# The second normalisation of a gated cross-attention and expert kernel by ScalarE, router logits in column groups, and five changes of order around them

## The chip, the cores and the metric

One core of a Trainium2 chip runs the kernel as one program. Its engines are TensorE (PE, matmuls and transposes; PEld is its weight load), VectorE (DVE), ScalarE (ACT), GpSimd (POOL) and SyncE (SP), which here only issues DMAs. Each runs its own list of instructions in order and waits on semaphores for the others. The metric is the time of the whole program on the device in microseconds.

## What is computed

For 16 sequences of 256 tokens of width 256, `x` is first changed by gated cross-attention to a context, and then by a gated layer of experts. From the reference, with the settings of the parts left out:

```python
x = x + tanh(g_xattn) * attention(layernorm(x), ctx, ctx, Wq, bq, Wk, bk, Wv, bv, Wo, bo)   # 16 heads of 16
x = x + tanh(g_ffn) * experts(layernorm(x), ...)

logits = xf @ w_router                                   # 8 experts
scores = softmax(logits); weights, indices = top_k(scores, 2)
y = (silu(xf @ w1[e]) * (xf @ w3[e])) @ w2[e]            # hidden width 512
moe_out = sum over the two experts of weight * y
shared = (silu(xf @ ws1) * (xf @ ws3)) @ ws2
out = shared / 3 + moe_out * 2 / 3
```

## The kernel before

Every large product is made of three matmuls on a high and a low part of its operands (`high*high`, `low*high`, `high*low`), so each tensor that goes into a matmul is first split: ScalarE copies the high part, VectorE or GpSimd subtracts and leaves the low part.

**Attention** is software-pipelined over the sequences, called batches here: b0 to b15. In iteration i (from -4 to 15) batch i+4 (`Eb`) is read and its first normalisation is begun, i+3 (`A`) is projected to k, q and v, i+2 (`F`) goes through DRAM and comes back as rows of `q4` and `k4`, for i+1 (`B`) the row maxima of the scores are found, i (`C`) has its scores again and their exponentials, i-1 (`S`) is divided and turned, i-2 (`S2`) is projected out, added to `x` and normalised a second time, i-3 (`S3`) is routed, and i-4 (`S4`) gets its places in the lists of the experts. An iteration has eight slots p = 0 to 7, each for one pair of heads: on TensorE four matmuls of scores for the exponential (`scores_to_exp`), four for the maximum (`scores_to_max`), and then that slot's share of the other stages. VectorE takes one `row_max` of 128 by 1024 in each slot, with `before(p)` ahead of it and `behind(p)` after it; ScalarE takes one exponential of 128 by 1024 (L953) in each slot, with a `before` and a `behind` too. The order in each slot is written out by hand, and nothing reorders it.

What the change touches in an iteration:
- `logits` (L705, slot 1): eight matmuls of 128 rows by 8 columns of output into bank `T1`. On VectorE `best_two` in slot 2 finds the two best experts, and `masks` (L1265 to L1269) behind that slot's `row_max`. `rank` (L715, L716, slot 3) counts into `T2`, and `positions` (L1273) reads the counts behind slot 4.
- `residual` (L1299), `residual_stats` (L1231) and `residual_variance` (L1237, L1242) of `S2` in slots 4 and 5 on VectorE; the root of the variance (L1653) on GpSimd; `norm` (L1314, two `tensor_scalar` of 128 by 256) on VectorE in slot 7; `turn_norm` (L650) on TensorE at the end of slot 7.
- `turn_max` (L681) turns the 16 maxima per token in slot 0, ScalarE negates them into `mT` (L1008), and SyncE writes them as the 64th row of each half of `q4`.
- GpSimd subtracts the mean of `Eb` (L1707), multiplies by the root (L1710), then takes the root of `S2` and leaves the low part of q (`leave_low`, L1685).

**The ramp** (i < 0) has no work of later stages; there TensorE also runs `keep_warm`, matmuls whose output nobody reads (L604). SyncE's list (`half_out` stores q or k of a batch to DRAM, `terms_in` reads them back) is written out for the first three batches.

**Behind the iterations** stands a tail for b14 and b15, woven into tiles 0 to 5 of the shared expert. Then tiles 6 and up: at most 48 routed tiles (it depends on the routing) of 256 tokens, in loops, and the rest of the shared tiles, mixed into the output. `scatter` writes each token's normalised row to the lists of its two experts in DRAM (`xs_d`), and `clear_behind` (L341) writes 512 rows of zeros behind each list's end, 514 KB for each of eight lists. SyncE clears list 0, reads the first routed tile, clears 2, 4 and 6, and reads the second tile; GpSimd clears 1, 3, 5 and 7 (counted on `z_pool`). SyncE reads a tile with four DMAs (`load_tile`, L442); `turn_rows` (L1422) on VectorE turns it, and `xg_h` and `xg_l` are its two parts. Only the first four routed tiles are read before all of the clears are known to be done.

## Time and profile of the kernel before

| | |
|---|---|
| median of three runs | 816.92 us (815.06 to 818.07) |
| the profiled execution's own time | 814.12 us |
| its span, granted clock of TensorE | 812.4 us, 0.992 of full speed |
| busy: TensorE, weight load | 769.9 us (95%), 686.5 us (85%) |
| busy: VectorE, ScalarE, GpSimd | 538.8 us (66%), 413.4 us (51%), 430.7 us (53%) |
| chain that ended last | PE 61%, POOL 10%, DMA 9%, issue 7%, DVE 7%, ACT 4% |

The busy share is an average over stages that differ. In the trace the first exponential scores of batch i mark iteration i: the ramp takes about 60 us, the iterations in the middle some 20 to 21 us each up to about 355 us, the tail and the first shared tiles last to about 425 us, the routed tiles to about 700 us, and the remaining tiles to the end. The time of a part is read as the distance between the same instruction in two iterations, and a loss as the idle time that stands in brackets at the instruction that waited.

### The profile page before, as it was taken

The page shows a single profiled execution, that of the slowest core. Times are in us where ns is not written, and L with a number is a line of the kernel's source. Part 1 is how long each engine was busy: PE and PEld are TensorE (multiplying, and loading weights), DVE is VectorE, ACT ScalarE, POOL GpSimd, SP SyncE. Part 2 cuts the span into 40 slices and gives each one's busy share as a digit, 9 for nine tenths or more (in the row PEclk, how much of TensorE's full clock was granted, in tenths as well). Part 3 has the DMA queues.
Part 4 walks back from the last instruction along what each step waited for, and adds up shares of the span by engine and source line. Part 5 has one row for each costly group of instructions (what it writes and reads, how often), then busy time and mean ns, then how long its engine had stood idle before and what let it go on. Part 6 is the DMA issues. An engine that isn't in the chain of part 4 may idle for free.

```text
span 812.4 us, 19406 instructions
## 1 busy us (share of the span) xinstructions
PE 769.9 (95%) x6955; PEld 686.5 (85%) x6956; DVE 538.8 (66%) x1118; ACT 413.4 (51%) x690; POOL 430.7 (53%) x489
## 2 busy tenths in 40 slices
PE   4888999999999998898997999999999999999998
PEld 3756777777777776578997999999999999999998
DVE  5677889998888888857644444444444444446897
ACT  5667777777777767653324333333334334333332
POOL 5633446666666654457772476656756675236000
PEclk9999999999999999999998999999999999999999
DMA  6854557776666654244394354444543422317622
GB/s 213 272 179 158 173 185 231 234 235 209 210 209 209 198 182 145 93 170 138 110 248 113 96 155 130 117 114 131 142 116 78 111 70 58 72 53 306 233 93 79
DMA packets 129150, 127.34 MB, mean 157 GB/s; under 512 B 55232, under 2 KB 111040, under 8 KB 129088
## 3 DMA queue, kind: packets, MB, share of 16 engines
q1 hardware_dynamic: 114896, 80.34, 33.4%
q0 software_dynamic: 14192, 46.19, 16.9%
q8 instruction: 37, 0.61, 0.3%
q14 instruction: 25, 0.20, 0.1%
HBM read 75.32 MB, written 50.91 MB: 155 GB/s over the span
## 4 chain that ended last, share of the span: by engine, by line
PE 61%; POOL 10%; DMA 9%; issue 7%; DVE 7%; ACT 4%; SPq 2%; POOLq 1%; ACTq 0%; DVEq 0%
PE bank L562 7%; PE bank L563 6%; PE bank L564 6%; PE bank L643 6%; PE bank_ss L614 6%; PE bank_sm L627 4%; POOL w_l L1635 4%; DMA y_d<-y_s,y_rows 3%; PE bank_sm L562 3%; PE bank_ss L562 3%; PE bank_sm L563 3%; PE bank_sm L564 3%; PE bank_ss L564 3%; PE bank_ss L563 3%; PE bank L650 3%
## 5 line engine op out<-in xcount | busy, mean ns | idle before, releaser
L1248 DVE TENSOR_REDUCE row_max<-bank_sm 128x4 f32<-128x1024 f32 x124 | 151.5, 1222 | 37.8 <-PE bank_sm L627 36.2
L953 ACT ACTIVATE probs_T<-bank_ss 128x1024 f32<-128x1024 f32 x123 | 126.5, 1028 | 18.9 <-PE bank_ss L614 17.9
L1227 DVE TENSOR_TENSOR gT_l<-gg,gT_h 128x1024 fp32r<-128x1024 f32 x49 | 66.8, 1363 | 102.0 <-ACT gT_h L1084 100.1
L562 PE MATMUL bank_sm<-xg_h,w_h 128*128 128x256 f32 x400 | 114.3, 286 | 7.1 <-DVE xg_l L1227 7.1
L562 PE MATMUL bank_ss<-xg_h,w_h 128*128 128x256 f32 x400 | 113.2, 283 | 0.5 <-DVE gg L1434 0.5
L563 PE MATMUL bank_sm<-xg_h,w_l 128*128 128x256 f32 x400 | 113.6, 284 | 0.0
L564 PE MATMUL bank_sm<-xg_l,w_h 128*128 128x256 f32 x400 | 113.5, 284 | 0.0
L564 PE MATMUL bank_ss<-xg_l,w_h 128*128 128x256 f32 x400 | 112.9, 282 | 0.0
L563 PE MATMUL bank_ss<-xg_h,w_l 128*128 128x256 f32 x400 | 112.9, 282 | 0.0
L562 PE MATMUL bank<-w_h,gT_h 128*128 128x256 f32 x392 | 111.1, 284 | 1.5 <-DVE gT_l L1227 1.5
L563 PE MATMUL bank<-w_h,gT_l 128*128 128x256 f32 x392 | 110.9, 283 | 0.0
L564 PE MATMUL bank<-w_l,gT_h 128*128 128x256 f32 x392 | 110.7, 282 | 0.0
L1685 POOL TENSOR_TENSOR qk_s<-qk_s 128x512 fp32r<-128x512 f32 x32 | 41.8, 1307 | 108.9 <-ACT qk_s L994 108.9
L562 PEld LDWEIGHTS bank_sm<-xg_h,w_h 128*128 128x128 f32 x400 | 77.2, 193 | 8.1 <-DVE xg_l L1227 7.6
L1761 POOL DMA_INDIRECT y_d<-y_s,y_rows x68 | 73.5, 1081 | 17.1 <-issue 16.5
L563 PEld LDWEIGHTS bank_sm<-xg_h,w_l 128*128 128x128 f32 x400 | 77.2, 193 | 0.0
L564 PEld LDWEIGHTS bank_sm<-xg_l,w_h 128*128 128x128 f32 x400 | 77.1, 193 | 0.0
L562 PEld LDWEIGHTS bank_ss<-xg_h,w_h 128*128 128x128 f32 x400 | 76.3, 191 | 0.8 <-DVE gg L1434 0.8
L1078 ACT ACTIVATE sg<-bank_sm 128x512 f32<-128x512 f32 x98 | 53.2, 595 | 46.6 <-PE bank_sm L564 46.6
L994 ACT ACTIVATE qk_s<-bank,bqk_s 128x256 f32<-128x256 f32 (+1 forms) x128 | 53.5, 481 | 45.8 <-PE bank L564 45.8
L562 PEld LDWEIGHTS bank<-w_h,gT_h 128*128 128x128 f32 x392 | 74.8, 191 | 2.1 <-DVE gT_l L1227 2.1
L563 PEld LDWEIGHTS bank_ss<-xg_h,w_l 128*128 128x128 f32 x400 | 76.4, 191 | 0.0
(204 smaller groups left out, 1945.6 us busy)
## 6 DMA issues: line engine op xcount, KB each, us to landing
qk_d<-qk_s SPq DMA_DIRECT2D x64, 256.0 KB, 2.8
w_raw<-wall POOLq DMA_DIRECT2D x27, 512.0 KB
k<-qk_d SPq DMA_DIRECT2D x48, 256.0 KB
q<-qk_d SPq DMA_DIRECT2D x48, 256.0 KB
xq<-xs_d SPq DMA_DIRECT2D x140, 64.0 KB
y_pairs<-y_d POOLq DMA_DIRECT2D x16, 512.0 KB, 9.7
x<-x SPq DMA_DIRECT2D x16, 256.0 KB, 4.7
c_s<-ctxT SPq DMA_DIRECT2D x16, 256.0 KB, 3.1
```

The source lines that it names most:

```text
L562: pe.matmul(out, ah, bh, start=first and k == 0, stop=False)
L563: pe.matmul(out, al, bh, start=False, stop=False)
L564: r = pe.matmul(out, ah, bl, start=False, stop=last and k == n - 1)
L614: r = pe.matmul(exp_bank(V.b, pv)[:, par * 512 + half * L:par * 512 + (half + 1) * L], k4[V.slot][own, pv, half * P:(half + 1) * P], q4[V. ...
L643: r = pe.matmul(OT[g % 2][PVW * i:PVW * (i + 1), :], v_s[V.v_slot][:, kc, h, :], pT[:, h % 8, kc * L:(kc + 1) * L], start=kc == 0, stop=kc ...
L953: act.activation(pT[:, 2 * (pv % 4):2 * (pv % 4) + 2, :].rearrange("p h t -> p (h t)"), exp_bank(V.b, pv)[:, :], ACT.Exp, scale=D ** -0.5) ...
L994: r = act.activation(dst.bitcast(F32) if half else dst, bnk[:, oc * L:(oc + 1) * L], ACT.Identity, bias=bqk_s[:, 2 * side + oc:2 * side + ...
L1078: r = act.activation(sg[:, 2 * n:2 * n + 2, :].rearrange("p f t -> p (f t)"), psH1[n][:, :], ACT.Silu)
L1227: return v.tensor_tensor(dst, ps, high.bitcast(F32), ALU.subtract)
L1248: v.tensor_reduce(mx[B.slot][:, :, :].rearrange("p t (r q) -> p r t q", r=2)[:, :, :, p], max_bank(B.b, p)[:, :].rearrange("p (r t k) -> p ...
L1685: po.tensor_tensor(rest, rest.bitcast(F32), high.bitcast(F32), ALU.subtract).then_inc(done, 1)
L1761: po.indirect_dma_start(out=yd, out_offset=bass.IndirectOffsetOnAxis(ap=to[:, t:t + 1].bitcast(U32), axis=0), in_=y_s[:, t, :], in_offset= ...
```

## The change

- **The second normalisation** of batches 0 to 12 goes from VectorE to ScalarE: `x * rstd + shift`, an `Identity` with a pointer for scale and one for bias, behind slot 7. VectorE makes `-mean` (128 by 2) with the variance, GpSimd multiplies it by the root (`norm_terms`), and both of GpSimd's steps now stand between its subtraction and its multiplication for `Eb`. `turn_norm` goes to slot 0 of the next iteration.
- **The logits of batches 0 to 9** (iterations 3 to 12): the router's weights are padded to 32 columns and become the stationary side; four matmuls of 128 columns, one for each pair of chunk and token half, write four column groups of `T1`. ScalarE copies the bank (128 by 128), and one matmul by a matrix of zeros and ones (`C_SEL`) in slot 2 adds the halves and turns them back. `best_two`, `masks` and `rank` of these batches come a slot later, `rank` into `T0`; `attention_rows` in slot 5 then waits for `pos_ok`, which for all batches stood ahead of q's projection before.
- **The ramp**: of b0, GpSimd leaves the low part of q ahead of its multiplication, and SyncE reads q back ahead of b1's stores of k. The maxima of b0 are turned and written in two halves (`turn_first`, `first_max`, `first_rows`), and 14 + 4 + 4 matmuls of `keep_warm` become 4. The bias of the projection out is made an iteration earlier, a clear of `v` an iteration later.
- **The tail**: on VectorE the variance and `norm` of b14 stand ahead of b13's `positions`; GpSimd's order scatter, root, cut becomes cut, root, scatter (`cut` splits a part of the next expert weights).
- **The clears**: SyncE does all. Lists 1 and 2 are cleared where 2, 4 and 6 were, lists 3 to 7 one by one after every other routed tile in an unrolled part of its loop. GpSimd's clears go.

```diff
-CW = C_T3 + NST
+C_SEL = C_T3 + NST
+CW = C_SEL + TC * NX
+LW = P // (TC * EC)
+THIN = NB - AHEAD - 2
...
+            def first_rows(half):
+                sp.wait_ge(mT_ok, half + 1)
+                for par in range(2):
+                    row = ROWS * par + MROW
+                    sp.dma_start(q4[0][row:row + 1, HALF * half:HALF * half + HALF, :].bitcast(F32),
+                                 first_mT[half][par:2 * HALF:2, :].bitcast(F32)).then_inc((first_mrow, mrow)[half], 16)
...
             load_x(Batch(3))
+            terms_in(b0, 0)
             half_out(b1, 1)
-            terms_in(b0, 0)
             load_c(Batch(3))
+            terms_in(b1, 1)
             half_out(b1, 0)
-            terms_in(b1, 1)
             load_x(Batch(4))
             terms_in(b1, 0)
+            first_rows(0)
             half_out(b2, 1)
+            half_out(b2, 0)
+            first_rows(1)
             terms_in(b2, 1)
-            half_out(b2, 0)
-            max_rows(b0)
             terms_in(b2, 0)
...
-            clear_behind(sp, (2, 4, 6), z_done)
+            clear_behind(sp, (1, 2), z_done)
...
-            with sp.Fori(1, last3) as u:
+            for u in range(1, 2 * NX - 5):
+                if u % 2 and u > 1:
+                    sp.wait_ge(z_done, 16 * ((u + 3) // 2))
+                load_routed(u + 3)
+                load_rows(u)
+                if u % 2 and (u + 5) // 2 < NX:
+                    clear_behind(sp, ((u + 5) // 2,), z_done)
+            sp.wait_ge(z_done, 16 * (NX - 1))
...
+            def logits_apart(S3):
+                if among_first(S3, 1):
+                    pe.wait_ge(few_in, 64)
+                pe.wait_ge(xn2T_ok, S3.n(1, 1))
+                for j in range(TC * EC):
+                    t, k = j // EC, j % EC
+                    r = pe.matmul(lgT_p[LW * j:LW * (j + 1), :], wr_s[:, k, :], xn2T[:, k, t * P:(t + 1) * P], start=True, stop=True)
+                r.then_inc(lgT_ps, 1)
+
+            def logits_joined(S3):
+                pe.wait_ge(lgT_ok, S3.n(1, 1))
+                pe.matmul(lg_thin, lgT_s[:, :], K[:, C_SEL:C_SEL + TC * NX], start=True, stop=True).then_inc(lg_ps, 1)
...
-                        keep_warm(SS[:, 0:512], 14)
-                    if B and B.b == 1 and p == 1:
                         keep_warm(SS[:, 0:512], 4)
+                    if B and among_first(B, 1) and p == HALF + 1:
+                        pe.wait_ge(xnTl_ok, A.n(1, 1))
+                        turn_first(0)
                     if B:
                         scores_to_max(B, p)
+                    if p == 0 and C and among_first(C, 1):
+                        turn_first(1)
                     if p == 0 and C and not among_first(C, 1):
                         turn_max(C, S2)
+                    if p == 0 and S3 and by_scalar(S3):
+                        turn_norm(S3)
                     if p == 0 and S:
                         values(S, 2)
                     if p == 1 and S3:
-                        logits(S3, lg_p)
+                        (logits_apart if thin(S3) else logits_whole)(S3)
...
                         values(S, 3)
+                    if p == 2 and S3 and thin(S3):
+                        logits_joined(S3)
...
-                    if p == 3 and S3:
+                    if p == 3 and S3 and not thin(S3):
...
+                    if p == 4 and S3 and thin(S3):
+                        pe.wait_ge(xnTl_ok, A.n(1, 1))
+                        rank(S3, rk_thin)
                     if p == 4 and C:
...
+                        if S3:
+                            pe.wait_ge(pos_ok, S3.n(1, 1))
                         if C:
-                            pe.wait_ge(mT_ok, C.n(1, 1))
+                            pe.wait_ge(mT_ok, C.n(1, 2))
                         attention_rows(S)
                     if p == 5 and A:
...
-                        turn_norm(S2)
-                if B and among_first(B, 1):
-                    pe.wait_ge(mx_ok, PAIRS - 1)
-                    keep_warm(SM[:, 0:512], 4)
-                    turn_max(B, None)
...
+            def norm(S2):
+                act.wait_ge(shift2_ok, S2.n(1, 1))
+                moved(act, sc_done[1], S2.n(32, 32 - R * 32))
+                for t in range(TC):
+                    r = act.activation(xn2_s[S2.slot][:, t, 0:E], x2_s[:, t, :], ACT.Identity, bias=shift2[:, t:t + 1], scale=rstd2[:, t:t + 1])
+                r.then_inc(xn2_ok, 1)
...
+            def logits_turned(S3):
+                act.wait_ge(lgT_ps, S3.n(1, 1))
+                moved(act, lg_ps, S3.n())
+                act.activation(lgT_s[:, :], lgT_p, ACT.Copy).then_inc(lgT_ok, 1)
...
-                    if p == 0 and C:
-                        act.wait_ge(mT_ps, C.n(1, 1))
+                    if p == 0 and C and among_first(C, 1):
+                        first_max(1)
+                    if p == 0 and C and not among_first(C, 1):
+                        act.wait_ge(mT_ps, C.n(1, 2))
+                        act.wait_ge(first_mrow, 32)
                         moved(act, mrow, C.n(32))
                         act.activation(mT[:, :], mT_p, ACT.Copy, scale=-1.0).then_inc(mT_ok, 1)
+                    if p == HALF + 1 and i == -1:
+                        first_max(0)
...
+                    if p == 7 and S2 and by_scalar(S2):
+                        norm(S2)
...
+                if mv is bmv2:
+                    v.tensor_scalar(mean2[:, :], mv[:, :, 0], -1.0, None, ALU.mult)
                 v.tensor_scalar(mv[:, :, 1], mv[:, :, 1], 1e-5, None, ALU.add).then_inc(done, 1)
...
-                    if p == 2 and S3:
+                    if p == 2 and S3 and not thin(S3):
                         best_two(S3, lg_p)
+                    if p == 3 and S3 and thin(S3):
+                        best_two(S3, lg_thin)
...
-                    if p == 2 and S3:
+                    if p == 2 and S3 and not thin(S3):
                         masks(S3)
                     if p == 3 and A:
                         v.wait_ge(xnTh_ok, A.n(1, 1))
                         low(xnT_l[:, :, :], bank_chunks(T0), xnT_h[:, :, :]).then_inc(xnTl_ok, 1)
+                    if p == 3 and S3 and thin(S3):
+                        masks(S3)
...
             residual_stats(x14)
+            residual_variance(x14)
+            norm(x14)
             positions(x13, rk_tail)
-            residual_variance(x14)
             list_slots(x13)
             divide(x15)
-            norm(x14)
...
+                def norm_terms():
+                    root(bmv2, rstd2, var2_ok, S2, rstd2_ok)
+                    if by_scalar(S2):
+                        po.wait_ge(rstd2_ok, S2.n(1, 1))
+                        po.tensor_tensor(shift2[:, :], mean2[:, :], rstd2[:, :], ALU.mult).then_inc(shift2_ok, 1)
...
+                    if A and among_first(A, 1):
+                        leave_low(0, qh_ok, ql_ok)
+                    if S2:
+                        norm_terms()
                     po.wait_ge(rstd1_ok, Eb.n(1, 1))
                     po.wait_ge(xc_ok, Eb.n(1, 1))
                     po.tensor_tensor(xn_s[:, :, :], xn_s[:, :, :], rstd[:, :].unsqueeze(2).to_broadcast([P, TC, E]), ALU.mult).then_inc(xn_ok, 1)
...
-                    root(bmv2, rstd2, var2_ok, S2, rstd2_ok)
-                if A:
+                if S2 and not Eb:
+                    norm_terms()
+                if A and not among_first(A, 1):
                     leave_low(0, qh_ok, ql_ok)
                 if i == NB - 1:
...
-            scatter(Batch(NB - 4), 1)
             po.wait_ge(oh_ok, x13.n(1, 1))
             po.wait_ge(exp_ok, NB * PAIRS)
             po.wait_ge(mx_ok, NB * PAIRS)
+            cut(1, 0, which=(0,))
             root(bmv2, rstd2, var2_ok, x14, rstd2_ok)
-            cut(1, 0, which=(0,))
+            scatter(Batch(NB - 4), 1)
             scatter(x13, 0)
             scatter(x13, 1)
```

What this does to the lists of instructions, at three places. **VectorE, slots 2 to 5 of iteration 3** (S3 is b0; `row_max_1` are the maxima, `xnT_l` a low part for q, `one_hot` to `mask_total` the masks, `x2_s` the residual, `list_pos` the positions). Before:

```order
L1248 TENSOR_REDUCE row_max_1<-bank_sm 128x2x2 [waits sm_ps]
L1265 TENSOR_TENSOR one_hot<-consts,logits_order 128x32 [waits lgc_ok]
L1268 TENSOR_TENSOR mask<-one_hot 128x16 [waits chain]
L1269 TENSOR_TENSOR mask_total<-mask_total,mask 128x8 [waits chain]
L1248 TENSOR_REDUCE row_max_1<-bank_sm 128x2x2 [waits sm_ps]
L1227 TENSOR_TENSOR xnT_l<-bank6,xnT_h 128x512 [waits xnTh_ok]
L1299 SCALAR_TENSOR_TENSOR x2_s<-bank7,gate_tanh,x_0 128x512 [waits x2_st,xb_ok,op_ps]
L1248 TENSOR_REDUCE row_max_1<-bank_sm 128x2x2 [waits sm_ps]
L1231 BN_STATS bn_st2<-x2_s 128x6 [waits x2_ok]
L1231 BN_STATS bn_st2<-x2_s 128x6
L1273 TENSOR_TENSOR list_pos<-bank5,consts 128x16 [waits rk_ps]
```

After, from slot 3 on:

```order
L1344 TENSOR_REDUCE row_max_1<-bank_sm 128x2x2 [waits sm_ps]
L1321 TENSOR_TENSOR xnT_l<-bank6,xnT_h 128x512 [waits xnTh_ok]
L1361 TENSOR_TENSOR one_hot<-consts,logits_order 128x32 [waits lgc_ok]
L1364 TENSOR_TENSOR mask<-one_hot 128x16 [waits chain]
L1365 TENSOR_TENSOR mask_total<-mask_total,mask 128x8 [waits chain]
L1395 SCALAR_TENSOR_TENSOR x2_s<-bank7,gate_tanh,x_0 128x512 [waits x2_st,xb_ok,op_ps]
L1344 TENSOR_REDUCE row_max_1<-bank_sm 128x2x2 [waits sm_ps]
L1325 BN_STATS bn_st2<-x2_s 128x6 [waits x2_ok]
L1325 BN_STATS bn_st2<-x2_s 128x6
L1369 TENSOR_TENSOR list_pos<-bank6,consts 128x16 [waits rk_ps]
```

The masks moved from behind slot 2's maximum to behind slot 3's and the low part, right ahead of the residual.

**TensorE, slots 4 and 5 of the same iteration** (`bank_ss` and `bank_sm` are the scores, L643 / L682 the values, L659 / L698 `attention_rows`). Before, from the end of `rank`, which stands ahead of slot 4's scores:

```order
L716 MATMUL bank5<-mask,counters 128x16
L614 MATMUL bank_ss<-q4_1,k4_1 128x256 [waits exp_ok]
L614 MATMUL bank_ss<-q4_1,k4_1 128x256 x3
L627 MATMUL bank_sm<-k4_2,q4_2 128x256 [waits mx_ok]
L627 MATMUL bank_sm<-k4_2,q4_2 128x256 x3
L643 MATMUL bank4<-probs_T,v_0 32x256 [waits ot_ok,exp_ok,vr_ok]
L643 MATMUL bank4<-probs_T,v_0 32x256 x7
L614 MATMUL bank_ss<-q4_1,k4_1 128x256 [waits exp_ok]
L614 MATMUL bank_ss<-q4_1,k4_1 128x256 x3
L627 MATMUL bank_sm<-k4_2,q4_2 128x256 [waits mx_ok]
L627 MATMUL bank_sm<-k4_2,q4_2 128x256 x3
L659 MATMUL bank6<-consts,oT_1 128x128 [waits mT_ok,ot_ok,x2_ok,xnTl_ok]
```

After:

```order
L666 MATMUL bank_sm<-k4_2,q4_2 128x256 [waits mx_ok]
L666 MATMUL bank_sm<-k4_2,q4_2 128x256 x3
L777 MATMUL bank6<-mask_total,counters 128x16 [waits acc_ok,oh_ok,xnTl_ok]
L778 MATMUL bank6<-mask,counters 128x16
L682 MATMUL bank4<-probs_T,v_0 32x256 [waits ot_ok,exp_ok,vr_ok]
L682 MATMUL bank4<-probs_T,v_0 32x256 x7
L651 MATMUL bank_ss<-q4_1,k4_1 128x256 [waits exp_ok]
L651 MATMUL bank_ss<-q4_1,k4_1 128x256 x3
L666 MATMUL bank_sm<-k4_2,q4_2 128x256 [waits mx_ok]
L666 MATMUL bank_sm<-k4_2,q4_2 128x256 x3
L698 MATMUL bank6<-consts,oT_1 128x128 [waits mT_ok,pos_ok,ot_ok,x2_ok,xnTl_ok]
```

`rank` moved behind both groups of scores of slot 4 and ahead of the values, and `attention_rows` waits for `pos_ok` as well.

**SyncE, in the ramp**, from the stores of b0's q on (`q4_0` are b0's rows of q; the two stores with `k_high_ok` and `kl_ok` are those of b1's k). Before:

```order
L396 DMA qk_d<-qk_s 128x2x256 [waits q_high_ok]
L396 DMA qk_d<-qk_s 128x2x256 [waits ql_ok]
L363 DMA x_3<-x 128x2x256 [waits var1_ok]
L396 DMA qk_d<-qk_s 128x2x256 [waits k_high_ok,k_high_st]
L396 DMA qk_d<-qk_s 128x2x256 [waits kl_ok,k_low_st]
L407 DMA q4_0<-qk_d 32x8x256 [waits q_high_st,q_zero0]
L407 DMA q4_0<-qk_d 32x8x256
L407 DMA q4_0<-qk_d 32x8x256 [waits q_low_st]
```

After:

```order
L416 DMA qk_d<-qk_s 128x2x256 [waits q_high_ok]
L416 DMA qk_d<-qk_s 128x2x256 [waits ql_ok]
L383 DMA x_3<-x 128x2x256 [waits var1_ok]
L427 DMA q4_0<-qk_d 32x8x256 [waits q_high_st,q_zero0]
L427 DMA q4_0<-qk_d 32x8x256
L427 DMA q4_0<-qk_d 32x8x256 [waits q_low_st]
L416 DMA qk_d<-qk_s 128x2x256 [waits k_high_ok,k_high_st]
L416 DMA qk_d<-qk_s 128x2x256 [waits kl_ok,k_low_st]
```

The three reads of b0's q moved ahead of the two stores of b1's k.

## Rows read from the trace of the kernel before

**Rows 1.** Timeline (start, length, instruction, idle before, releaser): VectorE and TensorE at tile 7.
```profile
429.05 0.73 DVE L1422 STREAM_TRANSPOSE bank<-xq 128x512 f32<-128x512 f32 x1 [10.19 <-DMA xq<-xs_d]
...
431.19 0.58 PE L562 MATMUL bank_sm<-xg_h,w_h 128*128 128x256 f32 x1 [6.10 <-DVE xg_l L1227]
```

**Rows 2.** Windows: length; busy PE, PEld, DVE, ACT, POOL (count); clock, DMA share, GB/s.
```profile
412.00:416.00 4.00, 4.00 (x36) 4.00 (x35) 2.70 (x5) 0.60 (x1) 2.89 (x3) 1.00 1.09 289
432.00:436.00 4.00, 4.00 (x24) 4.00 (x24) 2.43 (x8) 3.59 (x6) 0.00 (x0) 0.64 0.53 165
436.00:440.00 4.00, 4.00 (x36) 4.00 (x35) 1.79 (x6) 2.15 (x4) 0.00 (x0) 1.00 0.18 35
```

**Rows 3.** DMA issues with KB each and median us to landing: the clears.
```profile
xs_d<-zero_rows SPq DMA_DIRECT2D x4, 514.0 KB, 7.2
xs_d<-zero_rows POOLq DMA_DIRECT2D x4, 514.0 KB, 13.1
```

**Rows 4.** Waits between 431 and 700 us: total, times, longest.
```profile
ACT y_s L1094 <- DMA y_d<-y_s,y_rows: 59.7, 16, 5.2
```

**Rows 5.** Chain of waits, 20 to 32 us: start, length, what.
```profile
25.04 5.33 DMA q<-qk_d
```

**Rows 6.** Timeline of the ramp: GpSimd, then TensorE.
```profile
19.47 1.28 POOL L1685 TENSOR_TENSOR qk_s<-qk_s 128x512 fp32r<-128x512 f32 x1
...
30.42 0.51 PE L627 MATMUL bank_sm<-k,q 63*128 63x256 f32 x4 [1.56 <-DMA q<-qk_d]
...
41.33 1.19 PE L604 MATMUL bank_sm<-wt_h 128*128 128x512 f32 x4 [0.64 <-DVE row_max L1248]
```

**Rows 7.** Windows, columns as in rows 2: iterations 4, 8 and 12.
```profile
120.12:141.28 21.16, 20.56 (x210) 15.40 (x208) 19.40 (x48) 14.79 (x29) 14.21 (x17) 1.00 0.71 226
203.18:223.32 20.14, 19.77 (x210) 15.20 (x208) 17.98 (x48) 14.80 (x29) 13.29 (x17) 1.00 0.63 211
283.82:304.75 20.93, 20.12 (x210) 15.30 (x209) 18.51 (x42) 14.45 (x28) 10.78 (x14) 1.00 0.52 177
```

**Rows 8.** Timeline of TensorE, iteration 9, slots 1 and 5.
```profile
222.65 0.51 PE L614 MATMUL bank_ss<-q,k 64*128 64x256 f32 x4 [0.37 <-issue]
...
223.32 1.06 PE L705 MATMUL bank<-wr_s,xn2T 128*128 128x8 f32 x8
...
232.98 1.09 PE L659 MATMUL bank<-consts,oT 128*128 128x128 f32 x8
```

**Rows 9.** Timeline of VectorE, iteration 9, slots 2 to 5.
```profile
227.76 0.18 DVE L1265 TENSOR_TENSOR one_hot<-consts,logits_order 128x32 f32<-128x32 f32 x1
...
228.87 1.23 DVE L1248 TENSOR_REDUCE row_max<-bank_sm 128x4 f32<-128x1024 f32 x1 [0.52 <-PE bank_sm L627]
...
231.27 1.22 DVE L1248 TENSOR_REDUCE row_max<-bank_sm 128x4 f32<-128x1024 f32 x1
...
233.06 0.16 DVE L1273 TENSOR_TENSOR list_pos<-bank,consts 128x16 f32<-128x16 f32 x1
```

**Rows 10.** Timeline: VectorE beside GpSimd's work, and without (237.64).
```profile
135.29 1.70 DVE L1314 TENSOR_SCALAR xn<-x_s,bn_mv,rstd 128x256 f32<-128x256 f32 x2 [0.45 <-POOL rstd L1653]
...
237.64 0.73 DVE L1314 TENSOR_SCALAR xn<-x_s,bn_mv,rstd 128x256 f32<-128x256 f32 x2
...
293.98 1.72 DVE L1242 TENSOR_SCALAR bn_mv<-bn_mv 128x2 f32<-128x2 f32 x1
```

**Rows 11.** Timeline of ScalarE: two halves with one pointer; the maxima's copy.
```profile
205.78 0.84 ACT L994 ACTIVATE qk_s<-bank,bqk_s 128x256 fp32r<-128x256 f32 x2 [1.67 <-PE bank L564]
...
221.32 0.37 ACT L1008 ACTIVATE minus_max_T<-bank 16x256 fp32r<-16x256 f32 x1 [0.83 <-PE bank L681]
```

**Rows 12.** Timeline of the tail: VectorE, then TensorE.
```profile
364.08 2.45 DVE L1314 TENSOR_SCALAR xn<-x_s,bn_mv,rstd 128x256 f32<-128x256 f32 x2 [0.50 <-POOL rstd L1653]
...
366.58 0.66 PE L650 MATMUL bank<-consts,xn 128*128 128x128 f32 x4 [1.09 <-DVE xn L1314]
368.25 0.39 PE L562 MATMUL bank_sm<-xg_h,w_h 128*128 128x256 f32 x1 [1.01 <-DVE xg_l L1227]
```

85 lines of the change are left out of this document (55 added, 30 removed).

## The prediction

> **What bounds the kernel now.** I read the busy shares first: TensorE is busy 95% of the span and no other engine is over 66%. So time can come only from TensorE's idle stretches, its slow clock, and its own work. I then went through TensorE's timeline by stage. The largest idle stretch of the program is 6.10 us, ahead of the first matmul of the second routed tile [rows 1]. The ramp has a wait of 1.56 us at its first scores and shorter ones later [rows 6]. The tail has two of about 1 us [rows 12]. In the iterations TensorE is busy 19.77 us of 20.14 in iteration 8; iterations 4 and 12 take 21.16 and 20.93 [rows 7]. VectorE is busy 17.98 us of the same 20.14, most of it in row maxima that feed the next scores, so small delays there reach TensorE.
>
> All sums are made against the profiled execution's own 814.12 us, which is 2.80 under the median of 816.92. I add that back at the end.
>
> **The clears: -7.1.** VectorE turned the second routed tile 10.19 us late, because the tile's read had not landed; TensorE stood still until 431.19 [rows 1]. All eight clears were in the queues by then, eight times 514 KB, with a median landing of 7.2 and 13.1 us [rows 3]. The read was issued at about 413 behind them. After the change only three clears come ahead of it (lists 0, 1 and 2), all issued some 5 us or more before it. I expect the read to land at 417 to 420, against about 423 from which it would be in time, so the whole 6.10 goes. The clock also fell in the pause: in the four microseconds after, TensorE began 24 matmuls, and 36 in the four after those [rows 2]. That is 4 x 12/36 = 1.3 us lost, and about 0.4 more ahead of that window: 1.7. Together -7.8; with the landing late by a little, -6.
>
> The other five clears now go one by one between the reads of routed tiles. A clear keeps the DMA engines busy for about 1.8 us by the 289 GB/s that stand at 412 to 416, where the clears ran [rows 2] (an estimate: 514 KB over that rate), once in two tiles of 8.6 us. ScalarE there already waits for the results' writes, 59.7 us in 16 waits [rows 4], and this was no cost to TensorE, whose longest pause in that stage was 0.6 us; but the cushion is not shown to be large. I take +0.7 for the five, between 0 and +3.
>
> **The ramp: -3.9.** TensorE's first scores of b0 waited 1.56 us at 30.42 for the last read of q, which landed 5.33 us after its issue at 25.04 [rows 5, 6]. Ahead of it stood 14 `keep_warm`, which were over by then. The low part of q is left by GpSimd; the first half's subtraction at 19.47 took 1.28 [rows 6] and stood behind a multiplication, which the change puts after it. The reads also no longer queue behind two stores of b1's k, of 256 KB each. I estimate the last landing at 27.5: -2.9. At the end of b0's maxima TensorE ran four more `keep_warm` after an idle 0.64 [rows 6] and then turned the maxima; VectorE idled 0.4 us in the meantime. Both groups of matmuls go, and VectorE passes from b0's last maximum straight to b1's first: -1.0. What comes late next is the k of b3: ScalarE's copy overwrites what the store of b2's k reads, and that store now stands behind `first_rows(0)`. By the times of this trace it lands at 41.3 to 42, needed by 42.9, so it is just hidden. Bounds: -1.1 (only the GpSimd part) to -5.5 (with the clock, which fell for 3.6 us here, kept up).
>
> **Iterations 3 to 12: -2.8.** I walked iteration 9. On TensorE: `logits` took 1.06 us for eight matmuls [rows 8]. The four column groups have no row of their own. The nearest is four matmuls of 256 columns in two row groups, 0.51 [rows 6]; half the columns gives 0.25. I take 0.28, from 0.25 to 0.5. The joining matmul is one of eight such, a quarter of 1.06 at most: +0.25. So k's projection starts 0.64 earlier, and slot 3's scores 0.39 earlier.
>
> On VectorE the third maximum starts at 228.48 and not at 228.87, where it had idled 0.52 [rows 9]. The masks, 0.60 in all from 227.76 on [rows 9], move behind that maximum and the low part. They end at 230.82, the residual at 231.39, and the fourth maximum starts there and not at 231.27 [rows 9]. `rank` must wait for the masks: TensorE is ready for it at 230.55 and gets them at 230.85. Its lead falls from 0.60 to 0.06. Then `positions` ends at about 233.34, `attention_rows` waits for it until 233.40 and not 232.98 [rows 8]: +0.42. The idle 0.37 ahead of slot 1's scores [rows 8] takes most of that up. The period stays 20.2, and TensorE's saving is not cashed. In the six iterations like iteration 8 I take +0.2 in sum.
>
> Where the change pays is in iterations that VectorE disturbs. The 128 by 256 pair of `norm` takes 0.73 alone, but 1.70 beside a GpSimd subtraction at 135.29, after an idle 0.45 on the root [rows 10]. Iterations 4 to 6, in which GpSimd takes its longest operations, lasted 62.87 together (the first of them 21.16 [rows 7]); with the pair and its wait gone from VectorE I put them at 60.6, -2.3. In iteration 12 the small addition at 293.98 took 1.72 beside a GpSimd addition of 128 by 512 [rows 10]. GpSimd's own work in that stretch moves: 20.93 [rows 7] to 20.2, -0.7.
>
> ScalarE takes the norm. The nearest row is a pair of 128 by 256 with one pointer, 0.84 [rows 11]; I take 0.95. It stands behind slot 7, ahead of the copy of the maxima, which had idled 0.83 before it [rows 11], so it fits almost exactly. If it does not, slot 0's exponential comes later by what is over, 0.1 to 0.4 each. VectorE's new 128 by 2 operation costs 0.17 in slot 5; GpSimd's extra one lies where it idles. `turn_norm` only moves from slot 7 to slot 0. Sum: 0.2 - 2.3 - 0.7 = -2.8, from -7.8 to +1.
>
> The Trainium skill, in "Advanced Engine Details and Errata", section "Mode Summary", states that VectorE's faster modes and GpSimd hold a shared port against each other. The trace agrees with it: 0.73 alone and 1.70 beside GpSimd. By that rule the excess leaves with the norm, but the new small operation may pay it in its place, and iteration 12 would keep its 1.5.
>
> The same notes, "ScalarE: Activation LUTs", section "What ACT_TABLE_LOAD costs", give a price for an activation and for each pointer. By it the pair would take an estimated 1.08 us; the sum would be higher by at most 0.5.
>
> **Iterations 13 to 15: +0.4,** for `turn_norm` in slot 0 of the first of them and for the wait on `pos_ok`.
>
> **The tail: -1.6.** VectorE's norm of b14 took 2.45 us at 364.08 beside `cut`; TensorE waited 1.09 for it and 1.01 for the tile behind it [rows 12]. With the variance and the norm first, and `cut` done before, the norm ends by about 362.5, and both waits shrink to about 0.5 in all. Bounds -0.5 to -2.2.
>
> **Sum.** -7.8 + 0.7 - 3.9 - 2.8 + 0.4 - 1.6 = -15.0. 814.1 - 15.0 = 799.1, and with the 2.8 back **802**.
>
> **The rivals.**
> - *TensorE sets the pace of the iterations* (0.15). The saving of 0.5 us in ten iterations is cashed. For it speaks that TensorE is busy 98% of iteration 8; against it the walk above, where `rank` and `attention_rows` wait for VectorE. 802 - 5 = 797.
> - *The ramp gives nothing* (0.15). Without `keep_warm` the clock falls at b0's scores, or the read of q is slow from the traffic beside it, as its 5.33 us suggest. 802 + 3.9 = 806.
> - *The pause at the clears returns elsewhere* (0.10). The read of a routed tile, or the results' writes, queue behind a clear in the loop, and five tiles lose 1 to 1.5 us each; ScalarE's waits for those writes speak for it. 802 + 7 = 809.
> - *No gain that can be told* (0.06). Ramp and clears both fail: 802 + 3.9 + 7.8 = 814.
> - *Slower* (0.04). The chain masks, residual, fourth maximum, fifth maximum on VectorE becomes the bound, because `best_two` now needs a gap ahead of slot 3's maximum. VectorE has 2.2 us of idle time in iteration 8. If `best_two` misses its gap, the output projection waits too (it needs `lgc_ok`), and a full slot of about 2.5 us is lost. It decides from 1.5 us in each of ten iterations; at 2.5 it gives 802 + 2.8 + 25 = 830. Against it: the logits come half a microsecond earlier, and a whole slot lies between.
> - That the change does not do what it says can hold for the norm: if ScalarE is late for the maxima, the row-maximum chain starts late. It is priced above at 0.1 to 0.4 an iteration, +1 to +5, within the range.
>
> **How the numbers follow.** My forecast has 0.50. The range of 796 to 810 covers it with its own bounds (-6 to -7.8, 0 to +3, -1.1 to -5.5, -7.8 to +1) and the first three rivals, less their edges. A measurement of this kernel can tell about 0.5%, 4 us. Faster by more than that, under 812.8: 0.90; within: 0.06; slower: 0.04.
>
> **What would show it.** Right: no idle stretch ahead of the second routed tile and full clock behind it; b0's first scores at about 27.5; the same matmul 20.2 us apart in all of iterations 4 to 12, with waits of TensorE for `one_hot`/masks at `rank` and for `list_pos` at `attention_rows`; ScalarE's norm pair at 0.95; the tail's two waits under 0.6 together. Wrong: periods of 19.7 or less (then TensorE set the pace), periods over 20.5 (then VectorE's or ScalarE's chain did), a low clock between 25 and 40 us, or waits for reads in the first ten routed tiles.

## The result, and the profile after

The changed kernel takes 809.78 us (median of 7 runs, 807.48 to 813.55) against 816.99 us (7 runs, 815.06 to 819.48). The ratio is 0.9914, with a 95% interval of 0.9887 to 0.9941: 0.9% faster, where 1.8% was forecast. The profiled execution took 807.48 us (span 805.6) against 814.12 (span 812.4).

The gain is split by matmuls that stand in both programs. "Batch i" is the second group of scores for the exponential of batch i, in slot 3 of iteration i (batch 1's is what the expectations below call slot 1 of iteration 1); "tile" is the first matmul of that tile. A period is the distance between two such marks.

| stretch | before | after | change | forecast |
|---|---|---|---|---|
| start to batch 1 (ramp) | 66.03 | 66.55 | +0.5 | -3.9 |
| batch 1 to 2 | 18.49 | 18.53 | 0.0 | |
| batch 2 to 12 (iterations 3 to 12, nearly) | 204.07 | 204.37 | +0.3 | -2.8 |
| batch 12 to tile 0 | 69.47 | 69.87 | +0.4 | +0.4 |
| tile 0 to 4 (tail) | 41.08 | 40.39 | -0.7 | -1.6 |
| tile 4 to 8 (clears) | 42.40 | 34.42 | -8.0 | -7.8 |
| tile 8 to the last matmul | 367.84 | 368.50 | +0.7 | +0.7 |

The row behind batch 12 holds the rest of iteration 12. Measured from its slot 1 to the next one, that iteration went from 20.9 to 20.4 us: -0.5, where the forecast of -2.8 counted on -0.7.

The clears gave what was forecast, and the other parts together nothing. Here is the stretch of the changed kernel in which TensorE had stood still and run slowly [rows 1, 2]; the columns are length, busy PE, PEld, DVE, ACT and POOL, granted clock, DMA share and GB/s:

```profile
424.00:428.00 4.00, 4.00 (x35) 4.00 (x35) 2.12 (x4) 2.29 (x3) 2.81 (x4) 1.00 0.99 281
428.00:432.00 4.00, 4.00 (x36) 4.00 (x35) 2.72 (x11) 3.83 (x8) 0.00 (x0) 1.00 0.32 118
```

TensorE begins 35 and 36 matmuls in 4 us, at full clock. In the routed tiles ScalarE's waits for the results' writes grew from 59.7 us in 16 [rows 4] to 63.0 in 17, with no new pause of TensorE to be seen (0.47 us was its longest behind tile 8, 0.57 before):

```profile
ACT y_s L1188 <- DMA y_d<-y_s,y_rows: 63.0, 17, 5.1
```

**The ramp** after (timelines give start, length, instruction, and in brackets the idle time before it and its releaser):

```profile
28.52 0.51 PE L666 MATMUL bank_sm<-k,q 63*128 63x256 f32 x4 [2.95 <-DMA q<-qk_d]
...
40.67 0.50 PE L666 MATMUL bank_sm<-k,q 63*128 63x256 f32 x4 [1.76 <-DMA q<-qk_d]
...
42.50 0.51 PE L666 MATMUL bank_sm<-k,q 63*128 63x256 f32 x4 [0.98 <-DVE row_max L1344]
...
42.00:47.00 5.00, 4.50 (x26) 4.00 (x27) 2.77 (x9) 1.09 (x3) 0.00 (x0) 0.66 0.66 206
```

The last read of b0's q lands 1.9 us earlier than in [rows 5, 6], not 2.9. But TensorE then pauses again, ahead of b1's scores (40.67) for b1's q, and at 42.50 for VectorE, and 26 matmuls behind these pauses run at a mean clock of 0.66. In the kernel before this stretch had 33 matmuls and full clock:

```profile
42.00:47.00 5.00, 4.78 (x33) 3.20 (x33) 4.32 (x11) 0.61 (x2) 0.53 (x1) 1.00 0.60 187
```

The wait for b1's q comes from the new order of SyncE's list. The store of b1's q stands behind the read of b1's k now, where it stood ahead of it, and so the three reads of b1's q are issued 3.9 us later. Before, and after:

```profile
31.84 1.90 SPq L407 DMA_DIRECT2D q<-qk_d  x3
```
```profile
35.70 1.90 SPq L427 DMA_DIRECT2D q<-qk_d  x3
```

**Iteration 8 to 9** after, TensorE:

```profile
203.49 0.42 PE L764 MATMUL bank<-xn2T,wr_s 128*32 128x128 f32 x8
...
207.11 0.40 PE L769 MATMUL bank<-consts,logits_T 128*128 128x16 f32 x2
...
210.50 0.41 PE L666 MATMUL bank_sm<-k,q 63*128 63x256 f32 x4
211.15 0.25 PE L777 MATMUL bank<-mask_total,counters 128*128 128x16 f32 x1 [0.24 <-issue]
...
213.82 0.95 PE L698 MATMUL bank<-consts,oT 128*128 128x128 f32 x7 [0.38 <-issue]
```

(The program has four matmuls of logits in either kernel. With fp32 operands each stands as two in the trace, which is why the rows count eight, here and in [rows 8], and two for the joining one.)

VectorE at the same place, and ScalarE's norm:

```profile
210.45 0.18 DVE L1361 TENSOR_TENSOR one_hot<-consts,logits_order 128x32 f32<-128x32 f32 x1
...
210.88 0.17 DVE L1365 TENSOR_TENSOR mask_total<-mask_total,mask 128x8 fp32r<-128x8 f32 x1
...
213.45 0.16 DVE L1369 TENSOR_TENSOR list_pos<-bank,consts 128x16 f32<-128x16 f32 x1
...
220.32 1.15 ACT L1048 ACTIVATE xn<-x_s,shift,rstd 128x256 f32<-128x256 f32 x2
```

As forecast, the counts (L777) wait for the masks (`mask_total` at 210.88) and `attention_rows` (L698) for the positions (213.45 + 0.16). The first wait is 0.24, the second 0.38 (0.42 was forecast), and the idle 0.37 of [rows 8] is gone. But the period is 20.38, not 20.2, in each of the six between batches 6 and 12, where it was 20.17 before in all but the first. The windows of one period, before and after:

```profile
207.93:228.09 20.16, 19.79 (x210) 15.21 (x209) 18.03 (x48) 14.80 (x28) 13.34 (x16) 1.00 0.63 209
```
```profile
207.92:228.31 20.39, 19.77 (x212) 14.83 (x211) 17.21 (x47) 15.87 (x32) 13.39 (x17) 1.00 0.62 201
```

VectorE is busy 0.8 us less and ScalarE 1.1 more, and TensorE loses 0.2.

In iterations 4 to 6 the gain is 0.7 in all (62.14 against 62.88 from batch 4 to 7) and not 2.3, the period before them is 0.7 longer (20.91 against 20.19), and the one before that 0.8 shorter (19.41 against 20.17). VectorE no longer has a norm that GpSimd could hold up, but in iterations 3 and 5 a small operation now meets GpSimd's work, and the masks come late for the counts, which waited 0.76 us in iteration 3:

```profile
106.64 1.04 POOL L1813 TENSOR_TENSOR xn_s<-x,bn_mv 128x512 f32<-128x512 f32 x1
107.02 0.70 DVE L1361 TENSOR_TENSOR one_hot<-consts,logits_order 128x32 f32<-128x32 f32 x1
...
143.95 0.51 PE L651 MATMUL bank_ss<-q,k 64*128 64x256 f32 x4 [0.59 <-DMA q<-minus_max_T]
...
146.64 1.00 DVE L1357 TENSOR_TENSOR logits_less_max<-logits_sorted 128x16 f32<-128x16 f32 x1
147.57 1.21 DVE L1344 TENSOR_REDUCE row_max<-bank_sm 128x4 f32<-128x1024 f32 x1
...
146.33 1.28 POOL L1785 TENSOR_TENSOR qk_s<-qk_s 128x512 fp32r<-128x512 f32 x1 [4.49 <-ACT qk_s L1079]
...
149.99 0.25 PE L777 MATMUL bank<-mask_total,counters 128*128 128x16 f32 x1 [0.56 <-issue]
```

The 128 by 16 subtraction took 1.00 us in place of 0.15 (at 208.13, without GpSimd beside it), and the counts waited 0.56 in place of 0.24. In iteration 5 of this profile TensorE also waited 0.59 us for the row of the maxima to land (143.95). The run with the filled ramp, whose iterations have the same code, had the first of these waits (0.64) and not the second.

The Trainium skill ("Advanced Engine Details and Errata", section "Mode Summary") states that GpSimd and VectorE's two-port instructions block each other; of a `tensor_tensor` such as this one that section says nothing. The runs here show that the excess came and went with the overlap, and not whether a port is the reason.

### The profile page after: what moved, and what is told of

Read it like the earlier page. It is cut to its first block, busy times and chain, and to the rows that moved or that the text cites. A ratio compares the mean times of both kernels' runs of the same rounds, so it can differ in the third digit from the quotient of the medians.

```text
span 805.6 us, 19417 instructions
## 1 busy us (share of the span) xinstructions
PE 764.6 (95%) x6959; PEld 679.4 (84%) x6960; DVE 523.9 (65%) x1108; ACT 427.8 (53%) x727; POOL 428.3 (53%) x498
## 4 chain that ended last, share of the span: by engine, by line
PE 64%; DMA 10%; POOL 9%; issue 7%; DVE 6%; ACT 2%; SPq 1%; POOLq 1%; ACTq 0%; DVEq 0%
PE bank L597 7%; PE bank L682 7%; PE bank L598 6%; PE bank L599 6%; PE bank_ss L651 6%; PE bank_sm L666 4%; DMA y_d<-y_s,y_rows 4%; PE bank_sm L597 4%; PE bank_ss L597 3%; PE bank_sm L598 3%; PE bank_sm L599 3%; PE bank_ss L599 3%; PE bank_ss L598 3%; POOL w_l L1735 3%; PE bank L689 2%
## 5 line engine op out<-in xcount | busy, mean ns | idle before, releaser
L1867 POOL DMA_INDIRECT y_d<-y_s,y_rows x68 | 70.2, 1032 | 16.4 <-issue 15.9
L599 PEld LDWEIGHTS bank_ss<-xg_l,w_h 128*128 128x128 f32 x400 | 76.3, 191 | 0.0
```

The costliest lines, as they stand in the source:

```text
L599: r = pe.matmul(out, ah, bl, start=False, stop=last and k == n - 1)
L1867: po.indirect_dma_start(out=yd, out_offset=bass.IndirectOffsetOnAxis(ap=to[:, t:t + 1].bitcast(U32), axis=0), in_=y_s[:, t, :], in_offset= ...
```

## Experiments

All ratios are to runs of the kernel before on the same chip, with their 95% intervals. The medians of the kernel before were 815.4 (first four), 816.2 (next four), 812.9 (next three) and 816.4 (last).

### What carries the gain: the clears alone

```diff
 # the kernel before, with the change's SyncE loop
-            clear_behind(sp, (2, 4, 6), z_done)
+            clear_behind(sp, (1, 2), z_done)
...
-            clear_behind(po, (1, 3, 5, 7), z_pool)
```

> The kernel before with the change's clears alone. Theory (the clears carry the whole gain, the other parts together give nothing): the idle 6.10 us ahead of the second routed tile and the slow clock behind it go, routed tiles cost under 0.5 us more, so 814.1 - 7.7 = 806.4 for a profiled execution, median about 7.5 us under the kernel before. Rival (the other parts carry part of it): under 5 us.

Measured: 808.17 us, ratio 0.9914 (0.9882 to 0.9946), the same ratio as the whole change. Tile 4 to 8 took 34.41 us. So everything else in the change came to nothing in sum, to within what the two intervals leave (some 3.4 us). That sum hides parts of either sign. Against this profile, the changed kernel's ramp is 1.7 us shorter (66.55 against 68.27) and its tail 0.9 (40.39 against 41.26), but the stretch from batch 12 to tile 0 is 2.0 longer (69.87 against 67.90).

### The pauses in the ramp filled

```diff
-                        keep_warm(SS[:, 0:512], 4)
+                        keep_warm(SS[:, 0:512], 14)
+                    if B and B.b == 1 and p == 0:
+                        pe.wait_ge(mx_ok, PAIRS - 1)
+                        keep_warm(SM[:, 0:512], 3)
+                    if B and B.b == 1 and p == 1:
+                        pe.wait_ge(mx_ok, PAIRS)
+                        keep_warm(SS[:, 0:512], 4)
```

> The changed kernel with idle TensorE in the ramp filled: 14 instead of 4 keep_warm matmuls ahead of b0's first scores, 3 ahead of b1's and 4 ahead of b1's second. Theory (the missing keep_warm lets the clock fall behind the pauses at 38.9 to 42.5, which costs 1.3 us by 46 and 1.3 more by 60): full clock from 42.9 to 54, slot 1 of iteration 1 at about 64.5 instead of 66.5, total 2 us less than the changed kernel. Rival (the clock falls anyway, from load and not from pauses): as the changed kernel, or 0.5 us longer for the matmuls added.

Measured: 808.59 us, ratio 0.9935 (0.9901 to 0.9968), not to be told from the change. Half of the theory held. The windows 42 to 47 and 47 to 57:

```profile
42.00:47.00 5.00, 4.32 (x37) 3.24 (x37) 3.96 (x9) 2.25 (x6) 0.00 (x0) 1.00 0.66 219
47.00:57.00 10.00, 7.74 (x77) 5.02 (x74) 5.39 (x5) 6.51 (x12) 5.21 (x5) 0.83 0.66 215
```

37 matmuls at full clock in place of 26, and batch 0's mark comes at 46.56 in place of 47.77. Then the clock falls in the next stretch, and iteration 0 takes 19.63 us instead of 18.78; batch 1's mark is at 66.19 against 66.55. The rival is right on what it is worth. TensorE still waits for b1's q here, 0.59 us behind the added matmuls, and VectorE idles 1.03 ahead of b1's first maximum.

### The counts in another bank, the masks first

```diff
-                        pe.wait_ge(xnTl_ok, A.n(1, 1))
-                        rank(S3, rk_thin)
+                        pe.wait_ge(kh_ok, A.n(1, 1))
+                        rank(S3, rk_p)
...
-                        if S3:
-                            pe.wait_ge(pos_ok, S3.n(1, 1))
...
                         attention_rows(S)
...
+                    if p == 3 and S3 and thin(S3):
+                        masks(S3)
                     if p == 3 and A:
                         v.wait_ge(xnTh_ok, A.n(1, 1))
                         low(xnT_l[:, :, :], bank_chunks(T0), xnT_h[:, :, :]).then_inc(xnTl_ok, 1)
-                    if p == 3 and S3 and thin(S3):
-                        masks(S3)
```

> The changed kernel with the counts of the ten batches in bank T2 (free there since k was copied out), so that attention_rows need not wait for pos_ok, and with the masks ahead of the low part of the normalised rows. Theory (the two waits of 0.24 and 0.38 us in each of ten iterations are what eats TensorE's saving): both waits go, the period falls from 20.38 to 19.8, total 5 to 6 us less than the changed kernel. Rival (VectorE or ScalarE sets the period; the idle time only moves to the scores of a later slot): period 20.1 to 20.4, total within 2 us of the changed kernel.

Measured: 803.73 us, ratio 0.9855 (0.9806 to 0.9903). The period is 19.93 in all eight between batches 4 and 12, and batch 2 to 12 takes 199.70 us, 4.7 less than after. Both waits are gone, and one of 0.23 stands at the next scores, behind the row maximum that follows the masks:

```profile
209.46 0.51 PE L666 MATMUL bank_sm<-k,q 63*128 63x256 f32 x4 [0.23 <-DVE row_max L1342]
```

So waits were what kept the period at 20.38; the run "The counts in T2 alone" below shows that it was the one at `attention_rows`. What stands at 19.93 is the new wait for VectorE.

### The logits as before

```diff
-THIN = NB - AHEAD - 2
+THIN = 0
```

> The changed kernel with the logits, masks and counts of all batches as in the kernel before; the second normalisation stays on ScalarE and attention_rows keeps its wait, which is over by then. Theory (the logits' part costs, through its waits, more than its shorter matmuls save): TensorE does 0.4 us more of its own work, waits 0.6 less, period 20.0 to 20.2, total 2 to 3 us less than the changed kernel. Rival (the logits' part is worth its 0.4 us an iteration): period 20.6 or more, total 2 us or more above it.

Measured: 805.74 us, ratio 0.9886 (0.9854 to 0.9918). The period is 20.14 to 20.20 in all nine between batches 3 and 12, those of iterations 4 to 6 included; batch 2 to 12 takes 201.07, 3.3 less than with the logits' part. The norm by ScalarE without the logits' part thus gives 3.0 against the 204.07 of before, 2.4 of it in iterations 4 to 6 (60.44 against 62.88), where 2.3 was forecast. Iteration 12 went from 20.9 to 20.5. `attention_rows` still waits 0.38, now in vain, since the counts are in T2.

### The logits as before, without that wait

```diff
-THIN = NB - AHEAD - 2
+THIN = 0
...
-                        if S3:
-                            pe.wait_ge(pos_ok, S3.n(1, 1))
...
                         attention_rows(S)
```

> The logits, masks and counts of all batches as in the kernel before, the second normalisation on ScalarE, and no wait for pos_ok ahead of attention_rows (the counts are in T2, which attention_rows does not write). Theory (with the norm gone VectorE needs about 19.9 us an iteration and sets the period, whichever way the logits are made): the 0.38 us wait goes, period 19.9 instead of 20.14, within 1 us of the run with the counts in T2. Rival (TensorE sets it, and the column groups' 0.4 us are worth having): period 20.1 or more, since its own work is 0.4 us longer than there.

Measured: **799.09 us, ratio 0.9788 (0.9745 to 0.9831)**, faster than both kernels. The period is 19.71 to 19.73 in eight of the nine between batches 3 and 12 (batch 2 to 12: 197.48), less than the 19.93 that I took for VectorE's limit. The windows of one period with the logits' part (counts in T2), with the logits as before and the wait, and without:

```profile
204.49:224.42 19.93, 19.70 (x212) 14.82 (x211) 17.18 (x47) 15.80 (x32) 13.38 (x17) 1.00 0.59 197
```
```profile
204.06:224.20 20.14, 19.75 (x210) 15.27 (x209) 17.77 (x47) 15.69 (x30) 13.37 (x17) 1.00 0.62 202
```
```profile
204.76:224.48 19.72, 19.72 (x210) 15.27 (x209) 17.71 (x47) 15.47 (x30) 13.32 (x17) 1.00 0.63 207
```

In the last TensorE has no idle time at all: 19.72 of 19.72. Its logits take 0.3 us more than with the column groups, and it is still 0.2 faster. Two things make up the 0.5. The version with the groups waits 0.23 for the fourth row maximum, which costs 0.33 from start to start; my reading is that the masks behind slot 2 do not delay that maximum. And its counts cost 0.19 more where they stand. Behind slot 4's scores they take 0.14 and 0.18 us up to the next instruction, ahead of these scores, right behind the projection out, 0.03 and 0.18:

```profile
207.40 0.28 PE L777 MATMUL bank<-mask_total,counters 128*128 128x16 f32 x1
207.54 0.26 PE L778 MATMUL bank<-mask,counters 128*128 128x16 f32 x1
```
```profile
206.92 0.17 PE L777 MATMUL bank<-mask_total,counters 128*128 128x16 f32 x1
206.95 0.26 PE L778 MATMUL bank<-mask,counters 128*128 128x16 f32 x1
```

(The last 0.09 is in the projection ahead of them, whose last matmul takes 0.21 to the next start with the groups and 0.12 without.) My theory of 19.9 was too high, and the rival of 20.1 wrong.

A stop of TensorE costs more than its idle time. The same three instructions without a stop:

```profile
207.48 0.40 PE L666 MATMUL bank_sm<-k,q 63*128 63x256 f32 x4
207.80 1.07 PE L682 MATMUL bank<-probs_T,v 128*32 128x256 f32 x16
...
209.21 0.51 PE L666 MATMUL bank_sm<-k,q 63*128 63x256 f32 x4
209.65 0.55 PE L698 MATMUL bank<-consts,oT 128*128 128x128 f32 x3
```

From the scores to what follows it is 0.32 and 0.44 us here. In the changed kernel it is 0.65 (210.50 to 211.15) with an idle 0.24, and 0.89 with an idle 0.38: 0.09 and 0.07 more than the idle explains. (That the next matmul can't begin while the last one drains is my reading; no run separates it.)

### The norm back on VectorE

```diff
         def by_scalar(batch):
-            return batch.b < NB - 3
+            return False
```

> The changed kernel with the second normalisation of all batches on VectorE; the logits' part stays. Theory (the norm's move is what pays, the logits' part costs by its waits): iterations 4 to 6 at 21 or more again, the others at 20.2 to 20.6, 3 to 6 us more than the changed kernel. Rival (the norm's move is worth nothing): within 1 us of the changed kernel.

Measured: 808.96 us, ratio 0.9926 (0.99 to 0.9953), 1 us over the change by the ratio, not 3 to 6. But batch 2 to 12 takes 207.75, 3.4 more than after and 3.7 more than before. In this profile the ramp (66.24 against 66.55), the stretch from batch 12 to tile 0 (67.65 against 69.87) and the tail (39.36 against 40.39) were quicker and gave it back. The period:

```profile
209.19:230.02 20.83, 19.85 (x212) 14.78 (x211) 17.52 (x49) 15.06 (x30) 13.20 (x16) 1.00 0.62 202
```

20.83 with an idle 0.98: the waits at the counts and at `attention_rows` (0.23, 0.38), and the 0.37 of [rows 8] again, which with the norm on VectorE does not vanish. So the logits' part alone costs 0.66 us in each iteration.

### The tail

```diff
 # the clears-only kernel, and in the tail
             residual_stats(x14)
+            residual_variance(x14)
+            norm(x14)
             positions(x13, rk_tail)
-            residual_variance(x14)
             list_slots(x13)
             divide(x15)
-            norm(x14)
...
-            scatter(Batch(NB - 4), 1)
...
+            cut(1, 0, which=(0,))
             root(bmv2, rstd2, var2_ok, x14, rstd2_ok)
-            cut(1, 0, which=(0,))
+            scatter(Batch(NB - 4), 1)
```

> The kernel before with the change's clears and its tail. Theory (tail worth 1.1 to 1.7 us): from the first matmul of shared tile 0 to that of tile 4 39.4 to 40.4 us instead of 41.1 to 41.3, total 1.5 us under the run with the clears alone. Rival (the tail's waits only move): 41 us again. The run also gives one more look at the ramp of the kernel before, whose slot 1 of iteration 1 stood at 66.03 and 68.27 in two executions, and at 65.10 to 66.55 in four of the changed ramp; theory (the ramp change is worth about 1.2 us and the clock's falls there differ from execution to execution): between 66 and 68.5.

Measured: 804.33 us, ratio 0.985 (0.9806 to 0.9893). Tile 0 to 4 takes 39.37 us, against 41.08 and 41.26 without the tail: -1.8. (The ratio lies further below that of the clears alone, 0.9914, than this explains; their intervals overlap.) The ramp's mark was 67.57. In the profile of the changed kernel the same stretch took 40.39. There GpSimd's `cut` began late, since it stands behind a wait for b13's masks, and the root and the norm behind it:

```profile
359.53 1.04 POOL L1731 CAST w_h<-w_raw 128x1024 fp32r<-128x1024 f32 x1 [1.28 <-DVE mask_total L1365]
...
364.09 0.74 POOL L1753 TENSOR_TENSOR rstd<-bn_mv,power 128x2 f32<-128x2 f32 x1
...
367.53 0.66 PE L689 MATMUL bank<-consts,o_s 128*128 128x128 f32 x4 [1.24 <-issue]
```

Seven of the twelve profiles with this tail show 39.3 to 39.5, the others 40.0 to 40.4. In the seven `cut` begins 0.7 to 1.0 us ahead of tile 0's first matmul, in the five with it or up to 0.2 behind it. It is worth 0.7 to 1.9 us, on how the end of the iterations falls.

### The last iterations as before

```diff
 # on the version with the counts in T2 and the masks first
-            return batch.b < NB - 3
+            return batch.b < NB - 5
```

> The kernel with the counts in T2 and the masks first, and the second normalisation on ScalarE for batches 0 to 10 only, so that iterations 13 to 15 keep turn_norm in slot 7 as before. Theory (the pause of 1.5 to 1.8 us at the start of iteration 15 comes from turn_norm having left slot 7, and lets the clock fall for some 9 us in some executions): pause 1.0 or less, clock full from 334 to 344, 2 to 4 us less than with the counts in T2 alone, about 800 to 801. Rival (the clock's fall there is due to light load in the slots and comes with either order): same time, the clock low there in this profile too.

Measured: 801.48 us, ratio 0.9824 (0.9784 to 0.9864), against 0.9855 (0.9806 to 0.9903): the intervals overlap. The pause ahead of iteration 15 did shrink, from 1.48 us to 0.05, but the clock fell here too (0.63 from 338 to 342). For the version with all 13 batches on ScalarE the windows were:

```profile
334.00:338.00 4.00, 4.00 (x29) 2.18 (x27) 2.90 (x7) 2.80 (x5) 1.93 (x3) 0.53 0.19 70
338.00:342.00 4.00, 4.00 (x29) 2.48 (x29) 2.77 (x12) 2.15 (x4) 1.40 (x2) 0.50 0.18 66
```

29 matmuls in 4 us; batch 12 to tile 0 took 72.33 us there and 68.27 here, 69.47 before and 69.87 after.

### The ramp filled, on the fastest version

```diff
 # logits as before, no wait for pos_ok, and
-                        keep_warm(SS[:, 0:512], 4)
+                        keep_warm(SS[:, 0:512], 14)
+                    if B and B.b == 1 and p == 0:
+                        pe.wait_ge(mx_ok, PAIRS - 1)
+                        keep_warm(SM[:, 0:512], 3)
+                    if B and B.b == 1 and p == 1:
+                        pe.wait_ge(mx_ok, PAIRS)
+                        keep_warm(SS[:, 0:512], 4)
```

> The fastest version so far (logits and counts as before, norm on ScalarE, no wait for pos_ok ahead of attention_rows) with the ramp's pauses filled: 14, 3 and 4 keep_warm. Theory (in every profile without these matmuls the clock fell to 0.50 to 0.71 between 42 and 47 us, in the four with them it stayed at 1.00): clock 1.00 at 42 to 47, the second scores for the exponential of b0 at 46.5 to 47.5 instead of 48.87, total 1 to 2 us under that version. Rival (the fall only moves to 47 to 57): the clock is full at 42 to 47, but slot 1 of iteration 1 stands at 66 to 67 all the same, total within 1 us.

Measured: 802.09 us, ratio 0.9872 (0.9843 to 0.99), and so slower than without (0.9788, 0.9745 to 0.9831); the two ran on different chips, on which the kernel before stood at 812.87 and 816.16. Clock 1.00 from 42 to 47 and 0.83 from 47 to 57, as the rival has it; batch 1's mark is at 65.59. In iteration 15 this profile shows a long fall that the version without `keep_warm` did not have, in code that is the same. Batch 12 to tile 0 took 72.44 us, against 67.19 there:

```profile
334.00:338.00 4.00, 4.00 (x28) 3.07 (x30) 2.08 (x12) 2.66 (x4) 2.70 (x4) 0.50 0.32 119
338.00:342.00 4.00, 4.00 (x27) 2.97 (x18) 1.37 (x2) 1.50 (x3) 0.00 (x0) 0.50 0.06 19
```

### The counts in T2 alone

```diff
-                        pe.wait_ge(xnTl_ok, A.n(1, 1))
-                        rank(S3, rk_thin)
+                        pe.wait_ge(kh_ok, A.n(1, 1))
+                        rank(S3, rk_p)
...
-                        if S3:
-                            pe.wait_ge(pos_ok, S3.n(1, 1))
...
                         attention_rows(S)
```

> The changed kernel with the counts of the ten batches in T2 and no wait for pos_ok ahead of attention_rows; the masks stay behind the low part. Theory (the two waits add up): the 0.38 us at attention_rows go, the 0.24 us at the counts stay, period 20.38 - 0.45 + 0.0 to 0.1 = 19.9 to 20.05. Rival (the wait at the counts is the one that matters, the other would only move to the next scores): 20.3 or more.

Measured: 804.61 us, ratio 0.9911 (0.9876 to 0.9945), on a chip where the kernel before was at 812.87. Period 19.93 to 19.96 between batches 4 and 12: the wait for `pos_ok` is worth 0.43, and the order of the masks next to nothing. (Batches 2 to 12 took 199.51 us here and 199.70 with the masks first, and yet the ratios are 0.9911 and 0.9855, on two chips. Their intervals overlap, and a comparison of ratios across chips can be off by as much.)

### More filled in iteration 0

```diff
 # on the version with 14, 3 and 4 keep_warm
+                    if C and among_first(C, 1) and p in (3, 4):
+                        pe.wait_ge(qh_ok, R)
+                        keep_warm(T1[:, 0:512], (1, 5)[p - 3])
                     if V:
                         scores_to_exp(V, pv)
```

> As the version with 14, 3 and 4 keep_warm, and one and five more ahead of the second and third scores for the exponential of b0, where TensorE waits 0.4 and 1.3 us for ScalarE. Theory (the clock falls behind pauses): clock 1.00 from 47 to 57, iteration 0 takes 17.5 us, slot 1 of iteration 1 at 64 to 65, 1 to 2 us less than without these six. Rival (it falls there by chance of the execution, with or without a pause): the clock below 0.9 somewhere between 47 and 57 in this profile too, or total within 1 us.

Measured: 803.43 us, ratio 0.9887 (0.985 to 0.9924). From 42 to 56 the clock stayed full, then it fell:

```profile
47.00:57.00 10.00, 7.80 (x75) 4.98 (x76) 5.50 (x5) 6.56 (x12) 5.25 (x5) 0.95 0.64 215
57.00:63.00 6.00, 5.63 (x52) 4.27 (x54) 3.63 (x6) 3.49 (x7) 1.28 (x1) 0.80 0.15 50
```

Iteration 0 took 20.92 us, the longest of all. The rival is right: in all three profiles with filled pauses the fall of the clock came later, and it was not gone.

### The last iterations as before, on the fastest version

```diff
 # logits as before, no wait for pos_ok, and
-            return batch.b < NB - 3
+            return batch.b < NB - 5
```

> Logits and counts as in the kernel before, no wait for pos_ok ahead of attention_rows, and the second normalisation on ScalarE for batches 0 to 10 only, so that iterations 13 to 15 are those of the kernel before. Theory (iterations 13 to 15 lose 3 to 4 us in those executions in which the clock falls there, and it fell in most profiles with turn_norm moved and in fewer without): the two batches' norm back on VectorE shortens the pause ahead of iteration 15 to 1.0 us, and the total is 1 to 2 us under the version with all 13 on ScalarE (ratio to the kernel before 0.977 to 0.980, against 0.979 for that). Rival (the clock's fall there is a matter of the execution): ratio 0.979 or more, or a fall of the clock between 330 and 345 in this profile too.

Measured: 799.81 us, ratio 0.9811 (0.9783 to 0.984), the same as the 0.9788 of all 13 batches within their intervals. Its profile is the shortest seen (span 795.8), with full clock from 330 to 350, but so was that of the other (797.2). The pause ahead of iteration 15 was 0.50 us, against 1.01. The rival stands; that the moved `turn_norm` brings the fall of the clock in iteration 15 is not shown.

## Why the prediction was wrong

The forecast was 802 us, in a range of 796 to 810; the measured 809.78 is inside it, at its edge. The direction was right, and the size (15 us forecast, 7.2 measured) was not. Two terms failed: the ramp (-3.9 forecast) and iterations 3 to 12 (-2.8 forecast). By its own steps:

- **Clears, -7.1: right.** -8.0 between tiles 4 and 8, and +0.7 over all behind it. In the clears-only kernel nothing else changed, and it has the whole gain. One reading was loose: of the eight clears, those of lists 0 and 2 had landed (the latter at 409.62) when the read was issued at 412.85.
- **Ramp, -3.9: wrong by about 3,** and by 4.4 in the profiled pair. The landing of q was put at 27.5; b0's first scores came between 27.82 and 28.84 in the eight profiles of the changed ramp without filling, against 29.74 to 31.30 in three of the ramp before: -2.2 in the mean, not -2.9. Behind that, two things were missing.
  - *b1's q.* The forecast passed VectorE "straight" from b0's last maximum to b1's first, and named b3's k as what comes late next. But SyncE reads b1's q 3.9 us later, and in all eight profiles TensorE waits 1.76 to 3.70 us for it ahead of b1's first scores; in the three of the ramp before it has no such wait. VectorE idled 0.14 to 2.38 us ahead of b1's first maximum (1.2 in the mean), and 0.38 before. The filled ramps have the wait too, so it does not hang on the clock. b1's first scores start 1.5 us earlier in the mean (40.82 against 42.36), less than b0's. No run moved the store of b1's q back, so what it is worth is open.
  - *The clock.* In every one of those eight profiles the mean clock between 42 and 47 us was 0.50 to 0.71, and it was 1.00 in all six with more such matmuls in place (three of the ramp before, three filled). "Both groups of matmuls go" was booked as a gain of 1.0, and the fall of the clock only as a risk. But batch 1's mark lies at 66.3 in the mean of the three filled profiles too, the same as without filling, so the lost clock between 42 and 47 us alone is not what the ramp lacks.

  What is left at batch 1's mark is a mean of 66.3 (65.10 to 67.63, eight profiles) against 67.3 (66.03 to 68.27, three): -1.0, less than the marks differ among themselves. The single profile of before that I read, 66.03, was the luckiest of three.
- **Norm by ScalarE in iterations 4 to 6 and 12, -3.0: right by itself, lost in company.** With the logits as before, iterations 4 to 6 took 2.4 us less and iteration 12 0.4. I priced ScalarE's pair at 0.95; it took 1.08 to 1.15. The estimate of 1.08 by the Trainium skill ("ScalarE: Activation LUTs", section "What ACT_TABLE_LOAD costs") was the better one, and most pairs of the trace lie 0.06 above it. It did not delay the copy of the maxima, which still starts 0.04 us behind `turn_max`; the idle 0.83 ahead of that copy is gone.
- **Logits' part, +0.2 in the other iterations: mis-sized, and its combination missed.** The places of the two waits were right, and `rank` and `attention_rows` waited as the walk said. The shorter matmuls gave what was forecast: 0.36 from start to start for the logits, in place of 0.91, and 0.24 for the joining one. But the walk ended at 20.2 and the trace at 20.38. It gave no price to the new place of the counts (0.15 to 0.19) nor to what each stop costs above its idle time (0.07 to 0.09). And I compared with the period of before, in which an idle 0.37 stood that the norm's move takes away. Against what the rest of the change makes possible (19.72), the part costs 0.66 an iteration. The walk took "the idle 0.37 takes most of that up" as a gain of the logits' part, and it was the norm's: with the norm on VectorE and the logits' part kept, the 0.37 stays.
- **Iterations 4 to 6.** The forecast said that the small new operation might pay beside GpSimd; another small one did, 1.00 for 0.15, ahead of the masks. Of the 2.3, 1.6 were given back: some 0.5 by a period of 20.38 in place of 20.2 in each of the three, and 1.0 in iteration 5 by that operation and by the wait of 0.59 for the maxima.
- **Iterations 13 to 15, +0.4: right in this profile** (about +0.6, with the gain of iteration 12 taken out of its row), and too low over all of them. Batch 12 to tile 0 took 67.19 to 72.60 us in the eight profiles with `turn_norm` moved in these iterations, 70.4 in the mean, and 67.65 to 69.47 in the six without, 68.2 in the mean. In the eight TensorE pauses 1.0 to 1.8 us ahead of iterations 14 and 15, in the six 0.9 at most. Whether the clock falls there because of it is not shown.
- **Tail, -1.6: within its bounds,** at -0.7 in the profile and -1.8 by itself.
- **The rivals.** "TensorE sets the pace" (797) meant that the shorter logits are cashed. No version did that: with the counts in T2 the period is 19.93 to 19.96, and TensorE without any idle time, 19.72 and 799.1 us, comes with the logits as before. What came true was the rival that the ramp gives nothing (806), together with the lost 2.8 of the iterations. That the measured time still lies in the range is owed to its width; the clears alone give it.

Left open: what decides in which execution the clock falls in iterations 0 and 15. It fell with and without each edit that was tried.

## What to carry to other kernels

Before a result moves to another bank, ask who writes that bank next: putting the counts into T0 saved nothing and made `attention_rows` wait for VectorE, 0.43 us in each iteration, more than the shorter matmuls gave. Price each part of a bundled change against the version without only that part, and not against the kernel before; here the 0.44 us an iteration that the norm's move gives hid most of the 0.66 that the logits' part costs. When transfers in a list change places, follow each one that now comes later, not only the one that was pulled forward: the store of b1's q was such a one. And where the profile comes from one execution, compare the marks of several before a microsecond in a ramp is believed.

## What the runs showed of the hardware

- A fp32 `tensor_tensor` of 128 by 16 on VectorE took 1.00 us beside a GpSimd subtraction of 128 by 512, and 0.15 without; the norm's pair had gone from 0.73 to 1.70 [rows 10]. It ended at 147.64, when GpSimd's (146.33 + 1.28) did, and `one_hot` (107.02 + 0.70) with GpSimd's of 106.64 + 1.04: the delay was what was left of the other engine's operation.
- Four fp32 matmuls into four column groups (128 by 32 by 128; eight in the trace) took 0.36 us from the first's start to the next instruction, where four of 128 by 128 by 8 (eight in the trace too) took 0.91. In the trace the four groups start within 0.02 us of each other, the others 0.11 to 0.14 apart.
- A stop of TensorE cost 0.07 to 0.09 us more than the idle time that the profile shows for it, at two places of each iteration.
- Filling TensorE's pauses in the ramp kept the clock at 1.00 from 42 to 47 us in three profiles of three, and in each of them it fell within the next 16 us. Iteration 0 of the unfilled ramps took between 17.30 and 20.06 us, of the filled between 19.16 and 20.92.
